# Nested guards for the optional slots, a second PSUM pair for the second mix, a split load of one down operand, and ScalarE's roundings ahead of its copies in the first token group

## The reference

```
y   = cond_w[id]^T @ x                       # per sequence, 64 x 64
x1  = x + y @ W0^T + lora(gates(y), y)       # top 2 of 8 experts
z   = x1 @ W1[adapter]^T                     # per sequence, one of 8 matrices
q(w) = round(clip(w / (mean|w| + eps), -1, 1)) * mean|w|
out = x1 + ((z @ q(w_gate)^T) * (z @ q(w_up)^T)) @ q(w_down)^T   # inner width 2752
```

## Time and profile before

| | us |
|---|---|
| median of 3 runs | 1379.23 (1375.79 to 1380.08) |
| the profiled execution | 1379.09 |
| its span | 1377.5 |
| PE busy | 1326.7 (96%) |
| DVE busy | 727.0 (53%) |
| ACT busy | 409.9 (30%) |
| matmuls of the first group, L899 | 158.6 |
| transposes of the first group, L883 | 35.2, idle before them 9.7 |

### The profile page before, as it was taken

The page is one execution under the profiler, slowest core; times in us unless marked ns, Lnnn a source line. Parts: engine busy times, 40 slices in busy tenths (PEclk is TensorE's granted clock), DMA queues, the critical chain, the costliest instruction groups (busy, mean ns, idle before and its releaser), DMA issues.

```text
span 1377.5 us, 23462 instructions
## 1 busy us (share of the span) xinstructions
PE 1326.7 (96%) x8864; PEld 843.8 (61%) x8864; DVE 727.0 (53%) x1187; ACT 409.9 (30%) x456; POOL 141.8 (10%) x79
## 2 busy tenths in 40 slices
PE   5999999999999989999999999999999999999998
PEld 4566655454555544555444888844888845888843
DVE  5447656544543347888863455581455571555521
ACT  3445443232322437777720111120111110111100
POOL 3200000000000000000000123310222210233200
PEclk9999999999999999999999999999999999999999
DMA  9899999898829239999674633354544355444344
GB/s 250 283 382 351 352 355 259 250 311 271 238 81 196 87 118 312 335 331 331 208 282 175 226 137 136 143 219 176 194 160 159 123 203 196 169 154 160 138 187 145
DMA packets 171949, 302.48 MB, mean 220 GB/s; under 512 B 99008, under 2 KB 131008, under 8 KB 164064
## 3 DMA queue, kind: packets, MB, share of 16 engines
q1 hardware_dynamic: 159072, 263.76, 57.2%
q10 hardware_dynamic: 11776, 37.14, 7.6%
q0 software_dynamic: 1024, 0.53, 0.2%
HBM read 212.39 MB, written 68.03 MB: 204 GB/s over the span
## 4 chain that ended last, share of the span: by engine, by line
PE 73%; DVE 7%; DMA 6%; issue 5%; ACT 4%; SPq 2%; ACTq 1%; POOL 1%; POOLq 0%; DVEq 0%
PE pair L964 27%; PE pair L1001 15%; PE pair L844 11%; PE pair L762 11%; DMA region_q<-wb_scratch 3%; DMA wb_scratch<-region_q 3%; PE pair L899 2%; PE pair L730 2%; PE pair L677 2%; PE pair L745 2%; ACT region_q L1185 1%; PE pair L780 1%; ACT region_q L1201 1%; DVE region_q L1623 1%; SPq L500 1%
## 5 line engine op out<-in xcount | busy, mean ns | idle before, releaser
L964 PE MATMUL pair<-act_t,region_q 128*128 128x256 f16 x3696 | 404.0, 273 | 0.0
L964 PEld LDWEIGHTS pair<-act_t,region_q 128*128 128x128 f16 x3696 | 361.4, 98 | 42.8
L1001 PE MATMUL pair<-region_q,region_w 128*128 128x512 f16 x1232 | 269.1, 381 | 6.3 <-DMA region_q<-wb_scratch 6.0
L662 POOL TENSOR_TENSOR region_w<-region_q,region_w 128x1792 f32 (+1 forms) x33 | 118.4, 3587 | 1137.2 <-ACT region_w L1210 1137.2
L1001 PEld LDWEIGHTS pair<-region_q,region_w 128*128 128x128 f16 x1232 | 120.3, 98 | 154.0 <-DMA region_q<-wb_scratch 7.9
L844 PE MATMUL pair<-region_w,act_t 128*128 x816 | 181.7, 379 | 3.1 <-DVE act_t L1311 1.6
L762 PE MATMUL pair<-region_w,act_t 128*128 128x512 f16 x768 | 168.5, 379 | 0.0
L899 PE MATMUL pair<-act_t,region_q 128*128 128x512 f16 x704 | 158.6, 385 | 5.1 <-issue 5.1
L1216 ACT ACTIVATE region_q<-pair 128x512 f32<-128x512 f32 x33 | 19.7, 597 | 402.2 <-PE pair L964 402.2
L844 PEld LDWEIGHTS pair<-region_w,act_t 128*128 x816 | 79.8, 98 | 93.3 <-issue 4.3
L1311 DVE SCALAR_TENSOR_TENSOR act_t<-pair,act_t 128x512 f32 (+1 forms) x66 | 61.1, 946 | 142.2 <-ACT act_t L1033 142.1
(11 more groups left out here) (187 smaller groups left out, 1013.6 us busy)
## 6 DMA issues: line engine op xcount, KB each, us to landing
region_q<-wa_scratch SPq DMA_DIRECT2D x33, 1792.0 KB, 7.3
region_q<-wb_scratch SPq DMA_DIRECT2D x28, 1408.0 KB, 6.0
region_q<-in_L_cond_weight SPq DMA_DIRECT2D x40, 512.0 KB, 8.3
w1s_scratch<-region_q ACTq DMA_DIRECT2D x40, 512.0 KB, 5.9
wa_scratch<-region_q SPq DMA_DIRECT2D x22, 896.0 KB, 5.8
region_w<-in_L_ffn_w_gate SPq DMA_DIRECT2D x16, 688.0 KB, 8.8
wb_scratch<-region_q SPq DMA_DIRECT2D x11, 896.0 KB, 4.1
region_q<-in_L_ffn_w_gate SPq DMA_DIRECT2D x19, 512.0 KB, 5.6
```

The lines of the kernel that those rows point to most:

```text
L662: pool.tensor_tensor(at(iop[:, 1], u), st[s][:, 0:7], at(iop[:, 0], u), ALU.subtract)\
L964: mm = pe.matmul(bank(s_bank, b)[:, (1 - h) * HALF:(2 - h) * HALF], ring_a[s][:, h, o_a, k], moving[a], start=(opens and h == 1 and k == 0 ...
L1001: mm = pe.matmul(bank(s_bank, b), iop[:, a, p, o_a, tp * P:(tp + 1) * P], ring_b[r][:, p], start=(opens and p == 0 and a == 0), stop=(not ...
```

## The change

Six edits:

1. `mix(1)` writes `pair[1]` in PSUM instead of `pair[0]` (`mix_pair`), and no longer waits for `low_y(0)`. `gate(0)`, which writes `pair[1]` too, waits for `y_low` 2 instead of 1.
2. The three guards for the optional slots are nested instead of one behind the other, on PE, ACT and DVE.
3. `gate_up(1)` on PE goes ahead of the guards; with it `scale_gate(1)` and `round_q(3)` on ACT, `turn_a(2)` and `product(1)` on DVE.
4. The operand of j = 1 of `down` is loaded in two DMAs, rows 0 to 4 and 5 to 10, with a semaphore each. PE runs rows 0 to 4 for both halves of the tokens, then rows 5 to 10. SP issues one DMA more per group.
5. In the first token group ACT does `round_q(m+2)` ahead of `store_q(m+1)`. DVE's and PE's orders stay.
6. Two semaphores are joined into one (`totals_done`), to make room for `half_loaded`.

The core of the diff:

```diff
@@
+        def mix_pair(t):
+            return pair[1 if t == 1 else 0]
@@ sync: load_products
+                if q % 18 == 1:
+                    sp.dma_start(ring_b[0][:, 0:FIRST], wb_dram[o][:, 0:FIRST]).then_inc(half_loaded, 16)
+                    sp.dma_start(ring_b[0][:, FIRST:NP], wb_dram[o][:, FIRST:NP]).then_inc(step_loaded[0], 16)
+                    return
@@ tensor: mix, gate
-                wait_if(pe, y_low, t)
+                if t > 1:
+                    pe.wait_ge(y_low, t)
-                    mm = pe.matmul(pair[0][:, k * P:(k + 1) * P], x_nat[slot][:, k * P:(k + 1) * P],
+                    mm = pe.matmul(mix_pair(t)[:, k * P:(k + 1) * P], x_nat[slot][:, k * P:(k + 1) * P],
-                pe.wait_ge(y_low, t + 1)
+                pe.wait_ge(y_low, max(t + 1, 2))
@@ tensor: the optional slots
             linear_t(k - 1, 0)
+            gate_up(1, 1)
             pairs = field(pe, F_CUM, NADP - 1, NSLOT)
-            for n in range(k, NSLOT):
-                with pe.If(pairs > n):
-                    if n == k:
-                        pe.wait_ge(prod_done, 1)
-                    linear(n, n % 2)
-                    linear_t(n, n % 2)
+            with pe.If(pairs > k):
+                pe.wait_ge(prod_done, 2)
+                linear(k, (k) % 2)
+                linear_t(k, (k) % 2)
+                with pe.If(pairs > k + 1):
...
@@ tensor: down
-                    pe.wait_ge(step_loaded[r], 16 * (q // 2 + 1))
-                    for part in ((range(0, NP - 1), range(NP - 1, NP)) if j == 0 else (range(NP),)):
+                    if j == 1:
+                        pe.wait_ge(half_loaded, 16 * (g + 1))
+                    else:
+                        pe.wait_ge(step_loaded[r], 16 * (q // 2 + 1))
+                    cut = (NP - 1, FIRST, NP)[min(j, 2)]
+                    for part in (range(0, cut), range(cut, NP))[:2 if cut < NP else 1]:
+                        if j == 1 and part[0] > 0:
+                            pe.wait_ge(step_loaded[r], 16 * (q // 2 + 1))
@@ scalar: around the optional slots, and the loop of the first group
             high_z(k - 1)
+            round_q(3, 1, 1)
+            scale_gate(1, 1)
...
                     scale_gate(m - 1, (c - 1) % 2)
+                    round_q(m + 2, c % 2, 2 * i + c // 2 + 1)
                     store_q(m + 1, (c + 1) % 2, 2 * i + (c + 1) // 2)
-                    round_q(m + 2, c % 2, 2 * i + c // 2 + 1)
                     if c % 2 == 0:
                         high_inter(0, 2 * i + c // 2 - 1, (c // 2 - 1) % 2)
@@ vector
             low_z(k - 1)
+            turn_a(2, 0)
+            product(1, 1, 0, 0)
```

More of the change, by code:

```diff
@@ L284, in build_program @@
         gate_std = sem("gate_std")
-        counted = sem("counted")
+        totals_done = sem("totals_done")
         tmpw_transposed = sem("tmpw_transposed")
@@ L304, in build_program @@
         stat_step = sem("stat_step")
-        mean_done = sem("mean_done")
+        half_loaded = sem("half_loaded")
         scales_ready = sem("scales_ready")
@@ L441, in build_program @@
         W0_PAIR = (3, 1, 0, 2)
+        FIRST = 5
         INDEX_ALL = 7
@@ L807, in _ @@
                     pe.matmul(pair[1][:, 0:2 * E], ones[:, :], cnt[:, :, :].rearrange("p a b -> p (a b)"),
-                              start=True, stop=True).then_inc(counted, 1)
+                              start=True, stop=True).then_inc(totals_done, 1)
             pe.wait_ge(tmpw_ready, 1)
@@ L907, in _ @@
             pe.wait_ge(x1_ready, NT)
-            pe.matmul(pair[3][:, 0:3], ones[:, :], ssum[:, 0:3], start=True, stop=True).then_inc(mean_done, 1)
+            pe.matmul(pair[3][:, 0:3], ones[:, :], ssum[:, 0:3], start=True, stop=True).then_inc(totals_done, 1)
             linear(k - 4, 1)
@@ L924, in _ @@
             linear_t(k - 1, 0)
+            gate_up(1, 1)
             pairs = field(pe, F_CUM, NADP - 1, NSLOT)
-            for n in range(k, NSLOT):
-                with pe.If(pairs > n):
-                    if n == k:
-                        pe.wait_ge(prod_done, 1)
-                    linear(n, n % 2)
-                    linear_t(n, n % 2)
+            with pe.If(pairs > k):
[3 more added lines that the diff above has]
+                with pe.If(pairs > k + 1):
+                    linear(k + 1, (k + 1) % 2)
+                    linear_t(k + 1, (k + 1) % 2)
+                    with pe.If(pairs > k + 2):
+                        linear(k + 2, (k + 2) % 2)
+                        linear_t(k + 2, (k + 2) % 2)
             def token_op(g, o, k):
@@ L1006, in down @@
                                 mm.then_inc(dn_done if tp == 0 else step_done, 1)
-            gate_up(1, 1)
             turn_q(2, 0, 1, (2,))
@@ L1042, in y_part @@
                 act.wait_ge(y_done, t + 1)
[L1043 removed]
+                high(act_t[:, 0, :, t * P:(t + 1) * P], chunked(mix_pair(t)), ACT_SCALE).then_inc(y_high, 1)
             def tmp_part(t):
@@ L1257, in _ @@
             high_z(k - 1)
+            round_q(3, 1, 1)
+            scale_gate(1, 1)
             pairs = field(act, F_CUM, NADP - 1, NSLOT)
[L1259 to L1264, removed]
+            with act.If(pairs > k):
+                copy_z(k, (k) % 2)
+                high_z(k)
+                with act.If(pairs > k + 1):
+                    copy_z(k + 1, (k + 1) % 2)
+                    high_z(k + 1)
+                    with act.If(pairs > k + 2):
+                        copy_z(k + 2, (k + 2) % 2)
+                        high_z(k + 2)
+            for m in range(2, 5):
+                if m > 2:
                     scale_gate(m - 1, (m - 1) % 2)
@@ L1267, in _ @@
                     store_q(2, 0, 1, (2,))
-                if m > 1:
-                    store_q(m + 1, (m + 1) % 2, (m + 1) // 2)
                 round_q(m + 2, m % 2, m // 2 + 1)
+                store_q(m + 1, (m + 1) % 2, (m + 1) // 2)
                 if m % 2 == 0:
@@ L1282, in _ @@
                 scale_gate(m - 1, (m - 1) % 2)
+                if m < IC - 2:
+                    round_q(m + 2, m % 2, m // 2 + 1)
                 if m < IC - 1:
                     store_q(m + 1, (m + 1) % 2, (m + 1) // 2)
-                if m < IC - 2:
-                    round_q(m + 2, m % 2, m // 2 + 1)
                 if m % 2 == 0:
@@ L1395, in low_y @@
                 v.wait_ge(y_high, t + 1)
-                low(act_t[:, 1, :, t * P:(t + 1) * P], ps8[0], ACT_SCALE, act_t[:, 0, :, t * P:(t + 1) * P])\
+                low(act_t[:, 1, :, t * P:(t + 1) * P], chunked(mix_pair(t)), ACT_SCALE, act_t[:, 0, :, t * P:(t + 1) * P])\
                     .then_inc(y_low, 1)
@@ L1495, in weigh @@
             def weigh():
-                v.wait_ge(counted, 1)
+                v.wait_ge(totals_done, 1)
                 gthen(v.tensor_scalar(okay[:, :, :], pair[1][:, 0:2 * E].rearrange("p (a b) -> p a b", a=2),
@@ L1806, in _ @@
             low_z(k - 1)
+            turn_a(2, 0)
+            product(1, 1, 0, 0)
             pairs = field(v, F_CUM, NADP - 1, NSLOT)
[L1808 to L1811, removed]
+            with v.If(pairs > k):
+                copy_z(k, (k) % 2)
+                low_z(k)
+                with v.If(pairs > k + 1):
+                    copy_z(k + 1, (k + 1) % 2)
+                    low_z(k + 1)
+                    with v.If(pairs > k + 2):
+                        copy_z(k + 2, (k + 2) % 2)
+                        low_z(k + 2)
             v.tensor_copy(z_nat[0][0:1, 0:1], mean[0:1, 0:1]).then_inc(slots_done, 1)
-            for m in range(1, 4):
-                if m > 1:
+            for m in range(2, 4):
+                if m > 2:
                     product(m - 1, (m - 1) % 2, (m - 1) // 2, (m - 1) // 2 % 2)
-                if m > 1:
-                    quantize(m + 2, m % 2, m // 2 + 1)
+                quantize(m + 2, m % 2, m // 2 + 1)
                 if m == 3:
```

2 lines of the change are left out of this document (1 added, 1 removed).

## The result

| | before | changed |
|---|---|---|
| median, us | 1377.51 (4 runs) | 1402.04 (4 runs, 1399.48 to 1404.45) |
| span of the profiled execution | 1377.5 | 1399.9 |
| ratio | | 1.0184, 95% interval 1.0165 to 1.0202 |

The change makes the kernel 1.8% slower: 24.5 us between the medians, 22.4 between the two spans. The forecast was 1401, with a range of 1391 to 1409.

What follows compares the result with a forecast made beforehand. PE was busy 96% of the span; the change would make a ScalarE-VectorE loop set the first group's period. 25.1 + 0.6 + 1.5 - 3.4 - 1.6 = +22.2 on 1379.09, so 1401 us, range 1391 to 1409.

Steps and rivals of the forecast that it cites:

- The loop: First token group: scale, product, clip, rounding, copies close a loop; period 17.74 to 20.88 us a pair, +25.1 us; chance 84%.
- about 2.3 and 5.1: Sign in the new profile: ACT's roundings wait for DVE's clips in every step, these many us in turn.
- Its ends: Start and end of the first group's loop: +0.6 us at the start, +1.5 at the end for a late `wb` store.
- The +0.6 ahead of `gate_up(4)`: Between `gate_up(1)` and `gate_up(4)`, two and a half steps already run in the new order and PE waits: +0.6 us.
- Guards: PE's 5.12 us idle ahead of `gate_up(1)`: one of three jumped-over guards stays, two thirds saved, -3.4 us.
- The dip that I counted as saved: Slow `gate_up` at 507.12 and 538.01, extra 1.65 us each from the clock; one of two saved, -1.6 us.
- Second mix: Start-up: `main(0)` can start about 1.9 us earlier, but `gate(0)` waits for the LoRA operand; 0, bounds -1.9 and +1.7.
- Split load: Down projection, j = 1: no gap there before, so 0; +0.4 us a group, 1.6 in all, if SP's queue were tight.
- Clock: Rival: PE's pauses dip the clock twice a chunk in the loop, +22 us, 1423 us; chance 6%.
- The roundings found no clips ready: Rival, first group: roundings find clips ready and never wait, PE becomes the bound, 1364 us; chance 6%.
- DMA did not set the 17.74: Rival: DMA traffic sets the loop's period, ACT's order doesn't matter, only guards count, 1375.7 to 1377 us; chance 4%.
- near 38: Sign in the new profile: PE's idle time ahead of the transposes, 9.7 us before, grows to near this many us.

Runs made afterwards that it cites:

- e1: Changed kernel with ScalarE's copies ahead of its roundings again, all other edits kept: 1374.03 us, ratio 0.9974 to the kernel before.
- e2: Kernel before with only ScalarE's roundings put ahead of its copies in the first token group: 1404.39 us, ratio 1.0196.
- e3: Changed kernel with quantize(m+2) ahead of product(m-1) on VectorE in the first token group: 1375.42 us, ratio 0.9994 to the kernel before.
- e4: Changed kernel with roundings first only in odd steps, copies first in even ones: 1381.83 us, ratio 1.0027 to the kernel before.
- e11: Changed kernel without VectorE's memsets that zero the unused half of the last chunk's tiles: 1399.66 us, ratio 1.0163 to the kernel before.
- e6: e1 with the three guards one behind the other again, gate_up(1) still ahead of them: 1373.77 us, ratio 0.9971 to the kernel before.
- e9: e8 with the second mix back on the first PSUM pair, behind low_y(0): 1364.71 us, ratio 0.9909 to the kernel before.
- e7: e1 with the operand of j = 1 loaded in one DMA and used in one piece: 1373.26 us, ratio 0.9956 to the kernel before.
- e8: Changed kernel with copies first, except that in odd steps the copy of kind 2 follows the roundings: 1365.66 us, ratio 0.9907 to the kernel before.
- e10: e9 with quantize(m+2) ahead of product(m-1) on VectorE: 1371.95 us, ratio 0.9954 to the kernel before.

## Why the prediction was right, and where it wasn't

PE at the places that the points below speak of, changed kernel. Around the guards:

```profile
501.91 7.07 PE L909 MATMUL pair<-act_t,region_q 128*128 128x512 f16 x32
510.56 0.61 PE L893 MATMUL pair<-ident,region_q 128*128 128x128 f16 x8 [1.58 <-issue]
513.17 2.74 PE L893 MATMUL pair<-ident,region_q 128*128 128x128 f16 x24 [2.00 <-DVE region_q L1845]
515.70 8.58 PE L909 MATMUL pair<-act_t,region_q 128*128 128x512 f16 x32
```

At the start:

```profile
29.21 10.53 PE L772 MATMUL pair<-region_w,act_t 128*128 128x512 f16 x48 [0.59 <-DVE act_t L1337]
...
44.24 5.14 PE L755 MATMUL pair<-region_q,act_t 128*128 128x160 f16 x48 [2.71 <-DVE region_q L1337]
49.22 10.52 PE L772 MATMUL pair<-region_w,act_t 128*128 128x512 f16 x48
```

The granted clock (the column behind POOL's busy time) right there, behind it, and in the last two `gate_up`:

```profile
44.00:49.00 5.00, 4.76 (x45) 4.76 (x46) 2.54 (x3) 0.30 (x1) 2.06 (x4) 0.66 0.76 284
49.00:60.00 11.00, 11.00 (x58) 5.43 (x56) 4.72 (x4) 5.75 (x7) 4.55 (x3) 1.00 0.79 273
703.00:710.00 7.00, 7.00 (x32) 3.35 (x32) 6.69 (x17) 4.81 (x5) 0.00 (x0) 0.75 0.09 30
```

- **The loop.** Right in kind and size. Period 20.88 worked out, 20.84 measured in the mean, and the 3.14 more than before is what was forecast; waits for clips "about 2.3 and 5.1", measured 2.20 and 5.04. e1, e2, e3 and e4 show that it is this loop: the loss comes and goes with edit 5, goes when the clips are taken out of it, and shrinks to the worked-out 18.1 (18.18) when one half is cut.
- **Its ends.** The term that was too small. I gave the end +1.5 for the late `wb` store and did not see the memsets in `quantize(21)`. They lie in the loop as well, since the roundings of chunk 21 wait for them: PE waits 3.95 at 701.12 instead of about 1.2. This is the 3.1 us by which `gate_up(20)` stands later than forecast (+23.84 against -3.4 + 0.6 - 1.6 + 25.1 = +20.7). From `gate_up(19)` to `gate_up(20)` it is 13.65 us (690.10 to 703.75), in e11 10.33, so the memsets cost 3.3 with what follows from them. The store's own share came in kind (a wait of 1.28 in e11, where I had 1.9); in the changed kernel a clock dip of 1.35 us in `gate_up(20)` hid it. The +0.6 ahead of `gate_up(4)` did not come: between 515.70 and 533.76 PE doesn't wait.
- **Guards.** I took -3.4 and said that `slots_done` is no new wait. It is one: PE waits 1.58 at the guard and then 2.00 for VectorE's copy (L1845), which now stands behind `product(1)`, and that waits for `scale_gate(1)`. `gate_up(1)` starts 5.21 us earlier; the two waits take much of that back, and the fewer waits of the next two chunks add to it. The dip that I counted as saved was not: it moved from `gate_up(1)` to the transposes at 513.17 (2.74 for 1.50) and to `gate_up(2)` (8.58 for 7.07). The other one (1.58, not 1.65) is gone from `gate_up(4)`, but the +25.1 was counted from the start of that `gate_up` and contains it already. The gain left at `gate_up(4)` is 4.25, near the -3.4 + 0.6 - 1.6 = -4.4 of the sum, by other parts than I gave, and that is luck. By e6 little of it is the nesting. The 108 ns for a compare-and-branch, from the Trainium skill ("Advanced Engine Details and Errata", Control Flow Timing), are too few for these guards here: two more cost 1.36 us in e6. My two thirds of 5.12 were too many. Whether the guards wait for a fetch, no run tests.
- **Second mix.** Forecast 0, with a bound of +1.7 for a clock dip. `main(0)` starts 2.7 us earlier (29.21 for 31.94), of which part is an earlier load; `gate(0)` waits 2.71, and its matmuls take 5.14 instead of 3.49, so that `main(1)` starts 0.60 later. That is the dip that I had named as a bound (1.65 of it), with the operand 1.05 earlier than before. Over all traces the edit costs about 1.7 (e9): the bound was nearer than the 0.
- **Split load.** No gain, as e7 shows.
- **Clock.** No lasting fall in the loop, so that rival is out. Two `gate_up` in it did run slower (8.76 at 648.46 and 8.44 at 669.58, for 7.07), but the two periods that hold them are 20.82 and 20.83 long: the waits took the dips in. In the first and third window above the granted clock is 0.66 and 0.75, a mean over time at 2.4 GHz and at 1.2 GHz; both follow a wait of PE (2.71 and 3.95 us), and neither stretch has idle time to absorb it. A long wait is no sure sign of a dip: in e3 3.74 us ahead of `gate(0)` were followed by none (3.49), and the two dips in the loop follow waits of 1.16 at most.
- **The other rivals.** The roundings found no clips ready: they wait in every step of the loop. DMA did not set the 17.74 either: e8 moves the same loads and stores in 16.49.
- **Behind the first group.** The forecast had no term for it; the changed kernel wins 2.2 back there (24.59 at `down(0)`, 22.4 at the end). 1.0 is the third wait ahead of j = 2, 1.42 now against 2.46; the rest fits the matmuls of the down projection, 267.6 us against 269.1, where before had a clock dip late in the last group. Both look like scatter; no run tests it.
- **Sum.** PE's idle time ahead of the transposes is 30.6 us (27.0 + 2.0 + 1.6), not "near 38": the forecast took 1.34 a chunk for the transposes, and in three pieces they are busy for 1.83 (3 times 0.61), which the profile doesn't count as idle. The total of +22.2 forecast against 22.4 between the spans is closer than its parts, and that is luck: the 3.1 missing up to `gate_up(20)` stand against the 2.2 won behind the group and the 0.75 that came where 1.5 was given for the store.

## What to carry to other kernels

An engine that waits has instructions queued behind it. Before a blocked instruction is put behind another one, ask what the other one waits for, and whether that follows from an instruction on the same engine in the same step: then the two waits don't replace each other, they close a loop that includes everything between them. Move only the one instruction that is blocked (e8: one copy of three, with the other edits 0.9% faster than before), and leave the work that is ready as a filler for the wait.

A loop's period can be worked out from one trace, from start-to-start distances: here 20.88 for 20.84, about 18.1 for 18.18, near 17.5 for 17.7; the first and last turns, with their special instructions, are where such a sum goes wrong.

## What the runs showed that was not expected

- Guards that are jumped over cost PE unlike amounts, each with reading the count: 5.12 us for three behind `linear_t`, 2.98 for three behind `gate_up(1)` (e6), 1.62 for one there (e1). Why the first is so much more stays open.
- Clips ahead of `product` helped where ScalarE's loop was the bound (e3), and cost 6 to 7 us where PE was (e10), since loads that land late then hold up the product.
